# Layer 0 of a Flamingo-style stack: the order of the first loads, ten row marks on ScalarE, and low weight parts behind the first two row gathers

## The reference

```python
x = x + tanh(g_xattn[0]) * moe(layernorm(x), ctx, Wg, bg, W1, b1, W2, b2)
# moe, for each of the 2048 tokens:
#   logits = ctx @ Wg + bg                      8 experts
#   top 2 of the logits, softmax over the two
#   y = sum over the two: weight * (relu(n @ W1[e] + b1[e]) @ W2[e] + b2[e])
```

## Time and profile before

| what | value |
|---|---|
| three runs | 758.37, 757.95, 753.97 us, median 757.95 |
| profiled execution, its own time | 758.14 us |
| span of its trace | 756.3 us |
| granted TensorE clock, mean | 0.947 of full speed |
| busy share PE, DVE, ACT, POOL | 87%, 76%, 70%, 42% |

### The profile page before, as it was taken

How to read it: one execution, slowest core, us unless ns; L and a number is a source line. 1 busy time by engine, 2 the same in 40 slices (tenths; PEclk the granted TensorE clock), 3 DMA queues, 4 the chain that set the end, 5 groups by cost and what they waited for, 6 DMA issues and landing times.

```text
span 756.3 us, 13768 instructions
## 1 busy us (share of the span) xinstructions
PE 655.7 (87%) x5031; PEld 451.2 (60%) x5039; DVE 572.8 (76%) x1105; ACT 525.6 (70%) x1074; POOL 319.4 (42%) x337
## 2 busy tenths in 40 slices
PE   6288999488997998998799999988999998888967
PEld 5167887233554554655795666546888686666622
DVE  5869997887898857998565888668973346666777
ACT  4775663567885764677438776747885689999877
POOL 4776675787766778881000000189930040000000
PEclk8579999799999999999799999989999999999998
DMA  8526482111110114410000000700000000000001
GB/s 301 173 57 181 130 136 70 49 45 35 38 38 25 33 51 76 66 38 12 1 1 1 0 1 1 281 2 1 2 1 1 1 1 1 1 0 1 1 0 55
DMA packets 40273, 36.11 MB, mean 48 GB/s; under 512 B 21800, under 2 KB 30256, under 8 KB 40208
## 3 DMA queue, kind: packets, MB, share of 16 engines
q1 hardware_dynamic: 33616, 21.73, 9.8%
q0 software_dynamic: 6592, 13.51, 7.6%
HBM read 30.11 MB, written 5.11 MB: 47 GB/s over the span
## 4 chain that ended last, share of the span: by engine, by line
PE 57%; DVE 19%; ACT 13%; issue 4%; DMA 3%; POOL 3%; SPq 0%; ACTq 0%; DVEq 0%; POOLq 0%
PE ps L1351 5%; PE ps L1567 4%; PE ps L1604 3%; PE ps L2073 3%; PE ps L1002 3%; PE ps L2337 3%; PE ps L2024 3%; PE ps L1595 3%; PE ps L213 2%; ACT big L2393 2%; PE ps L1585 2%; POOL pe L400 2%; PE ps L217 2%; PE ps L1031 2%; PE ps L1516 2%
## 5 line engine op out<-in xcount | busy, mean ns | idle before, releaser
L1497 POOL DMA_INDIRECT pe<-in_rpe,idx x128 | 135.0, 1055 | 35.7 <-issue 24.5
L1963 POOL TENSOR_SCALAR big<-big,wcols 128x256 f32<-128x256 f32 x1 | 0.9, 937 | 138.9 <-DMA big<-in_l3f_w 138.9
L384 POOL DMA_INDIRECT pe<-normed_rows,pe x46 | 48.6, 1057 | 20.2 <-issue 10.1
L525 ACT ACTIVATE pe<-ps,wcols 128x256 f32<-128x256 f32 x92 | 38.5, 476 | 22.4 <-PE ps L432 22.4
L1707 ACT ACTIVATE big<-ps,small 128x128 f32<-128x128 f32 x128 | 34.7, 382 | 17.5 <-PE ps L1595 17.5
L1212 ACT ACTIVATE big<-ps 128x1024 f32<-128x1024 f32 x32 | 32.6, 1019 | 18.1 <-PE ps L999 17.9
L1351 PE MATMUL ps<-nT,big 128*128 128x512 f16 x192 | 44.5, 379 | 0.0
L432 PE MATMUL ps<-big 128*128 128x256 f16 x276 | 36.8, 287 | 5.6 <-DVE big L578 4.4
L2337 PEld LDWEIGHTS ps<-big,pe 128*128 128x128 f32 x288 | 34.3, 192 | 11.9 <-ACT big L2385 5.9
L1232 DVE TENSOR_REDUCE small<-ps 128x16 f32<-128x1024 f32 x32 | 38.3, 1216 | 1.5 <-PE ps L993 1.5
L2337 PE MATMUL ps<-big,pe 128*128 128x128 f32 x288 | 35.5, 277 | 1.8 <-ACT big L2385 1.8
(11 more groups left out here) (429 smaller groups left out, 1971.2 us busy)
## 6 DMA issues: line engine op xcount, KB each, us to landing
pe<-in_l2f_w SPq DMA_DIRECT2D x16, 256.0 KB, 6.1
tile_results<-big SPq DMA_DIRECT2D x23, 128.0 KB, 2.2
pe<-in_xrow SPq DMA_DIRECT2D x4, 512.0 KB, 5.3
big<-in_l0x_w SPq DMA_DIRECT2D x8, 256.0 KB, 7.0
pe<-in_rpe,idx POOLq DMA_INDIRECT x128
cT<-in_cT SPq DMA_DIRECT2D x2, 512.0 KB, 4.6
nT<-in_l0x_w SPq DMA_DIRECT2D x4, 256.0 KB, 7.7
vx<-in_l0x_w SPq DMA_DIRECT2D x4, 256.0 KB
```

What stands on the lines that cost most here:

```text
L384: pool.indirect_dma_start(out=xg16[:, i % RX, h, :, :].rearrange("p r n -> p (r n)"), out_offset=None, in_=xrows_d, in_offset=bass.Indirec ...
L525: ins_ = act.activation(hid32[:, i % RF, f, :], hidden_ps(i, u)[:, f % 2, :], ACT.Relu, bias=wcols[:, bass.ds(at + (COL_AT["l0x_b1"][0] + ...
L1497: pool.indirect_dma_start(out=pe[:, v * D:(v + 1) * D], out_offset=None, in_=ins["rpe"], in_offset=bass.IndirectOffsetOnAxis(ap=idx[:, v:v ...
```

## The change

Five edits, all in layer 0:

1. SP issues the second half of the rows ahead of the two halves of the context.
2. ScalarE makes ten row marks, VectorE 22 instead of 24.
3. `row_f` gets a step of its own (`DVE_PLACE`), so ScalarE's marks may start at once after it instead of after `tile_of`. All later numbers of VectorE's steps move by one.
4. ScalarE writes the high parts of experts 0 and 1 after its marks instead of ahead of them.
5. After the two gathers of tile 0 GpSimd writes one column of a scrap tile and raises `s_set` to 7. VectorE waits for that before its low parts of experts 0 and 1, and GpSimd itself waits for it before its third gather.

```diff
-        DVE_STATS, DVE_COUNTS, DVE_LOGITS, DVE_PLACE, DVE_ROW = 0, 3, 4, 5, 5
-        ACT_ROWS = 8
+        DVE_STATS, DVE_COUNTS, DVE_LOGITS, DVE_PLACE, DVE_ROW = 0, 3, 4, 5, 6
+        ACT_ROWS = 10
...
-        POOL_SET, POOL_SHIFT = 4, 4
+        POOL_SET, POOL_SHIFT, POOL_FIRST = 4, 4, 7
...
@@ pool_layer0, in the loop over tiles, behind the two gathers of tile i
+                if i == 0:
+                    pool.memset(pause[:, 0:1], 0.0).then_inc(s_set, 1)
+                    pool.wait_ge(s_set, POOL_FIRST)
...
@@ act_layer0
             act.activation(z0, z0, ACT.Exp).then_inc(R0["act_step"], 1)
-            act_w_hi(act, 0)
-            act_w_hi(act, 1)
             act.wait_ge(R0["dve_step"], DVE_PLACE)
...
-            for e in range(2, 5):
+            for e in range(5):
                 act_w_hi(act, e)
...
@@ dve_route
-            link(dve.tensor_copy(row_f, row_i))
+            dve.tensor_copy(row_f, row_i).then_inc(R0["dve_step"], 1)
+            dve.wait_ge(R0["dve_step"], DVE_PLACE)
             link(dve.scalar_tensor_tensor(tile_f, place1, -1.0, row_f, ADD, SUB))
...
@@ dve_layer0
             dve_route(dve, link)
+            dve.wait_ge(s_set, POOL_FIRST)
             dve_w_lo(dve, 0)
             dve_w_lo(dve, 1)
...
@@ block.sync
+            x_rows(1)
             for h in range(2):
                 load("cT%d" % h, cT[:, h * 1024:(h + 1) * 1024], "cT", h * 1024)
-            x_rows(1)
             load("route", route, "route")
```

More of the change, by code:

```diff
@@ L296, in flamingo_kernel @@
         iota16, later16, ones16, ident16 = (half16[:, 128 * j:128 * (j + 1)] for j in range(4))
-        square16 = work[:, 4096:4608].bitcast(f16).rearrange("p (k n) -> p k n", k=ACT_ROWS)
+        square16 = work[:, 4096:4096 + 64 * ACT_ROWS].bitcast(f16).rearrange("p (k n) -> p k n", k=ACT_ROWS)
         hid32 = pe[:, 12288:14336].rearrange("p (s f n) -> p s f n", s=RF, f=FT)
```

## The result

The changed kernel takes 762.16 us (median of 9 runs, 758.9 to 763.27). The kernel before took 758.09 us beside it (9 runs, 753.97 to 758.78). The ratio is 1.0056, 95% interval 1.0038 to 1.0073: some 4 us slower, above the range of the prediction, and within the 1% that it called no change. The profiled execution took 761.04 us with a span of 759.2, against 758.14 and 756.3: 2.9 us more, at a mean clock of 0.942 against 0.947.

The account below looks back on a forecast made before the run. The chain was taken as almost all VectorE until the first gather, then the expert loop; starting up 1 1.05 us sooner (0.65 at the first gather included) gave 757.0 us, own range 756.3 to 757.7, 8 in 10: 753.4 to 759.2.

Parts of the forecast that it names:

- Part 1, order of loads: Layer 0 loads: rows' second half and context halves trade landing times, so routing starts at 12.85 us, 0.3 us sooner.
- The bounds: Range for routing's start after the reordered loads: from 0.95 us sooner to 0.5 us later, by the last context half's landing.
- the context lands late: slower: Rival at the context load: each microsecond behind 10.9 us takes one off the 1.05 us lead; chance 0.06.
- Part 2, the marks: Row marks before `gidx`: two fewer on VectorE save 0.46 us, TensorE gives back 0.12; net −0.35 us.
- Part 3: GpSimd up to the first gather of rows: ready in time, so that gather comes 0.65 us sooner, at 32.6 us.
- Part 4, the hold: Tile 0's gathers without low parts beside them: second gather 1.02 us shorter, a later one stretched; up 1 1.05 us sooner overall.
- the lead stays: Expert loop after up 1: VectorE's row has only small gaps, so the 1.05 us lead lasts.
- The rule to weigh: Skill's rule on VectorE disturbing GpSimd: low parts shouldn't slow gathers, so holding them back would bring nothing; the forecast followed the trace.
- The hold brings nothing: Rival at tile 0's gathers: stretching has another cause, up 1 at most 0.9 us sooner, 757.4 us; chance 0.10.
- The clock rises a tile later: Rival on TensorE in tiles 0 to 2: longer idling delays the high clock, costing 1.24 us per group, 758.1 or 759.4; chance 0.18.
- A tile sooner: Rival on TensorE in the first tiles: the high clock comes one tile earlier, 1.24 us more gain, 755.7 us; chance 0.13.

Follow-up runs that it names:

- kernel with more idle passes: Changed kernel with 33 instead of 20 idle products on TensorE ahead of the context's product: 759.88 us, ratio 1.0028.
- extra context half 1: Kernel before plus an unused 512 KB load of the context's second half ahead of the context; run once, read for landings, not time.
- extra rows half 0: Kernel before plus an unused 512 KB load of the rows' first half ahead of the context; run once, read for landings, not time.
- changed, split order: Changed kernel with the rows' second half loaded between the context's two halves: 757.77 us, ratio 1.0002; on the slow chip 884.2 us, ratio 0.9997.

## Why the prediction was wrong

**Part 1, order of loads,** is the step that failed, at "All three are 512 KB, so I let them change places: rows at 7.2 us, context at 8.5 and 10.9 us". The places don't trade times. Routing was forecast for 12.85 us and began at 17.04. The 4.2 us between them are about 2.1 of a later start and 2.1 of the clock:

- *The start of the product.* The rows' half landed at about 9, not 7.2, and the context's first half at 11.1, not 8.5. The step took its sum from the last half's landing alone, 10.9 us by the forecast and 12.4 measured, which by that sum costs 1.5 us. But with the first half 2.6 us late as well there is nothing to work on meanwhile, and all 32 passes, 3.65 us even at the high clock, lie behind its landing; that is another 0.6 us (11.21 + 3.65 + 0.1 = 15.0 us against 12.4 + 1.83 + 0.1 = 14.35). The kernel with more idle passes shows the start's part alone, routing at 14.72; the one with the context's first half in front has its last landing at 11.3 us and routing at 14.2.
- *The clock.* "That is 32 passes in 3.65 us" took the high clock as given. A wait of 3.2 us in front of them made it 5.71, one of 4.0 us 6.99. The kernel with more idle passes gave the 2.1 us back.
- *The bounds.* They ran from 0.95 us sooner to 0.5 later, measured: 3.9 later. The upper one took the weights' 7.7 us as landing time of a context half; the halves took 7.6 and 8.4. The landing was 0.7 us beyond the bound, and the rest of the miss is the product behind it. So a bound was taken from loads of another size, issued 7 us later.

The rival *the context lands late: slower* has the right mechanism. It was to decide from a landing at 11.95 us, and it landed at 12.4; but it priced the landing alone, one for one, and so would give 758.5 for what became 762.16. It had 0.06. Its evidence against, that "the weights' 7.7 us speak for 11.7 us at most", was a row of other loads at another time. The statement that the lead or lag of the first 40 us reaches the end held in the trace: 3.45 at the first gather, 2.9 at the end.

**Part 2, the marks,** was right: −0.35 us said, −0.43 and −0.36 measured, ScalarE with 1.0 us in hand, as said.

**Part 3** kept the 0.76 us between `gidx` and the first gather. They are there again (35.92 to 36.68), and GpSimd was ready ahead of `gidx`. Its 0.65 us sooner fell with part 1: the first gather is 3.45 us later.

**Part 4, the hold,** had its mechanism right down to the stretched third gather (1.81 us): tile 0's turn gained 0.97 us in the changed kernel, 0.96 and 0.98 in the two comparisons apart from it, where 1.02 was said. The sixth gather was said to gain 0.09 of its own, and gained 0.07 to 0.08. The next step, up 1 another 0.3 us sooner from ScalarE's copy, came out in size too: up 1 gained 0.62 us on the first gather in the changed kernel (2.83 late against 3.45) and 0.55 with the old loads, where 0.40 was said (1.05 less 0.65). What "the lead stays" has of it is seen when the traces are sorted by hold and by the clock at which up 1 ran (us; up 3 and the results' first gather are counted from the first gather of rows, to leave out what came earlier; the chip of 884 us is left out):

```
kernel                          hold   up 1 took   up 3    results
before                          no     2.74        18.11   89.54
extra context half 1            no     2.74        18.15   89.82
marks alone                     no     1.50        17.71   89.09
new loads alone                 no     1.50        17.59   89.36
extra rows half 0               no     1.50        17.74   89.09
changed                         yes    2.77        17.55   89.13
changed, old loads              yes    2.77        17.62   89.52
changed, more idle passes       yes    2.74        17.43   88.77
changed, split order            yes    2.71        17.45   89.09
hold alone                      yes    1.47        17.42   89.24
```

At up 3 the hold is still worth 0.5 to 0.7 us where up 1 ran at the low clock, and 0.2 to 0.3 where it ran at the high one. The 0.08 between "changed, old loads" and "marks alone" compares one of each. At the results the five kernels with the hold average 89.15 and the five without 89.38, and each group is spread over 0.7 us: what is left of the lead there, if anything, these traces can't tell.

**The rule to weigh.** The row decides against the inference: low parts with two SBUF inputs stretched the same gather to 1.97 us that takes 0.94 without them. Moving them moved the stretching too.

**The rivals.** *The hold brings nothing* is refuted in its mechanism; its time can't be told from the forecast's, since the hold alone has a ratio of 1.0006 (0.9986 to 1.0025), some 1.5 us to each side. *The clock rises a tile later* did not happen: up 1 ran at the low clock before and after (2.74 and 2.77 us), and up 2 took 1.78 us before, as the clock rose in its midst, and 1.47 after, where it had risen. *A tile sooner*, up 1 at the high clock, came in four of the ten kernels above, with and without the hold, so no edit here decides it. The prediction priced it at 1.24 us; without the hold it was worth 0.4 to 0.6 at up 3, which waits for VectorE's low part in any case (for 0.84 us in the kernel before, for 0.97 in the one with the marks alone). The loss of the clock that did count was one that no rival had, 35 us ahead of the place where I looked.

**The parts together.** Marks and hold were to bring about 0.4 us on the first gather and 0.4 more on up 1; with the old loads the traces show leads at the results' first gather of 0.8 us for both together and 1.3 for the marks alone, of which 0.5 is a routing that began sooner without being touched. The times can't tell: 1.0001 and 0.9997, with intervals of about 1 us to each side. No version that was tried beats the kernel before.

## What to carry to other kernels

When loads change places on a queue, don't let their times change places with them: take each load's own duration, ask for every consumer when its *first* piece comes and not only its last, and look for the one that works while the rest arrives. When the consumer is TensorE, add to its wait what the wait does to its clock, since passes behind a gap of 2 to 4 us cost up to twice as much; idle passes that last until the data are there avoid that, and a first piece that comes early avoids part of it. An operation that disturbs its neighbour disturbs the next neighbour when it is moved, so a hold is worth only what the displaced stretch doesn't take back a few steps on. And before two traces are compared for a small effect, look whether the clock was the same in both; here it differed by chance and covered most of what the hold was worth.

## What the runs showed of the hardware

- Loads of the same size in the same place of one queue took 4.6 and 5.4 us for halves of one table, 5.9 and 6.1 for halves of the other, and what follows was later by about as much. Only the pair of 4.6 and 6.1, on one chip, differs by more than the 0.4 to 0.7 us between kernels of one order.
- A gather that starts while a low part runs ends 0.8 to 0.9 us after that part's end (1.96, 1.97 and 1.81 us instead of 0.94), and the next low part doesn't hold it: in the changed kernel the third gather ends at 41.07 us, while the second low part runs until 41.38.
- TensorE's clock fell while it worked, in the midst of a product that stood behind a gap of 3.2 us: 13 passes at 0.114 us, then 19 at 0.223. After a gap of 1.8 us, 16 passes took 2.67 us instead of 1.86. The wait itself was spent at 1.00.
- In the one trace of the kernel with 26 more idle passes the last store took 4.2 us to land instead of 2.2, which took away what the passes had won.
- On one chip every kernel took 884 to 890 us, and one of 23 executions of the kernel before 2342. In the kernel with the hold alone 10.6% of the chain that ended last, 94 us, are waits that the profile puts down to another core or an unknown queue. The longest is VectorE's, 51.4 us ("remote"), and TensorE waits behind it. What they wait for is open (waits of that kernel: line, us in total, times, longest):

```profile
PE ps L1006 <- DVE xT L1279: 61.7, 6, 56.2
DVE xT L1279 <- remote: 51.4, 1, 51.4
```
